# Halved 64-wide joins, blocks placed by ScalarE and DMA, and a recut second inversion in a delta-rule block kernel

## The reference, cut to what matters

```python
qkv = x @ gates_w + gates_b
q, k, v = jnp.split(qkv, 3, axis=-1)
lr = x @ lr_w + lr_b
k = k / jnp.linalg.norm(k, axis=-1, keepdims=True)
K = jnp.tril(jnp.einsum('ntc,nsc->nts', k, k), k=-1)
A = K + jnp.eye(T, dtype=x.dtype)
u = jax.scipy.linalg.solve_triangular(A, v, lower=True)
score = jnp.einsum('nsk,ntk->nst', q, k)
y = jnp.einsum('nst,ntv->nsv', score, lr * u)
```

## Time and profile before

| | us |
|---|---|
| median of 3 runs | 202.74 (202.15 to 202.99) |
| the profiled execution | 201.71 |
| its span, first to last instruction | 199.8 |
| PE busy | 179.8 (90%) |
| DVE busy | 166.3 (83%) |
| ACT busy | 114.4 (57%) |
| mean granted PE clock | 0.993 of full speed |

### The profile page before, as it was taken

One profiled execution on the slowest core, in us unless ns is written; L12 is line 12 of the kernel. 1 busy time (PEld: TensorE's weight loads), 2 busy tenths in 40 slices (PEclk: granted clock), 3 DMA queues, 4 the chain that ended last, 5 costly groups with the idle time before them and its releaser, 6 DMA issues.

```text
span 199.8 us, 4189 instructions
## 1 busy us (share of the span) xinstructions
PE 179.8 (90%) x1299; PEld 130.7 (65%) x1299; DVE 166.3 (83%) x750; ACT 114.4 (57%) x318; POOL 63.7 (32%) x79
## 2 busy tenths in 40 slices
PE   0498799999999899999998999999999999999980
PEld 0355676887988677877864776766667675657540
DVE  7898899999899945494686688898989899878885
ACT  2567786588795785457327763645456363752420
POOL 8256980000000069980022220070605233202030
PEclk9999999999999999999999999999999999999997
DMA  4982011103000030000000000010101001011011
GB/s 115 302 211 29 10 16 20 21 5 59 3 2 3 0 61 1 3 3 3 0 2 0 3 0 0 0 54 3 53 0 36 18 5 53 0 53 53 0 54 53
DMA packets 20265, 6.53 MB, mean 33 GB/s; under 512 B 9995, under 2 KB 20244, under 8 KB 20244
## 3 DMA queue, kind: packets, MB, share of 16 engines
q1 hardware_dynamic: 19668, 6.21, 13.1%
q10 hardware_dynamic: 576, 0.07, 0.2%
HBM read 3.15 MB, written 2.10 MB: 26 GB/s over the span
## 4 chain that ended last, share of the span: by engine, by line
PE 62%; DVE 17%; ACT 5%; issue 3%; DVEq 0%; ACTq 0%
PE ps L1390 25%; PE ps L1104 10%; PE ps L1298 5%; PE ps L1099 5%; PE ps L1369 4%; DVE kT_all L1022 3%; DVE xi L836 3%; DVE prod L829 3%; PE ps L1133 2%; PE ps L1288 2%; DVE rv L885 2%; PE ps L1226 2%; PE ps L1282 2%; PE ps L1213 2%; PE ps L1116 1%
## 5 line engine op out<-in xcount | busy, mean ns | idle before, releaser
L1390 PE MATMUL ps<-ewC,kT_all 128*128 128x256 f32 (+2 forms) x192 | 62.0, 455 | 0.7 <-DVE kT_all L1022 0.7
L1022 DVE COPY_PREDICATED kT_all<-mask,ps 128x256 f32<-128x256 int32 x112 | 49.1, 439 | 2.6 <-DVE mask L1008 0.3
L1390 PEld LDWEIGHTS ps<-ewC,kT_all 128*128 128x128 f32 x192 | 33.9, 190 | 16.6 <-issue 6.0
L359 POOL TENSOR_TENSOR x_all<-x_all,kT_all 128x512 f32<-128x512 f32 (+1 forms) x8 | 9.6, 1204 | 54.6 <-ACT kT_all L679 54.6
L836 DVE TENSOR_TENSOR xi<-xi,prod 128x60 f32<-128x60 f32 (+13 forms) x116 | 19.6, 207 | 0.3
L829 DVE TENSOR_TENSOR prod<-lts,xi 128x60 f32<-128x60 f32 (+13 forms) x116 | 19.3, 204 | 0.3
L353 POOL TENSOR_TENSOR x_all<-x_all,h_all 128x512 f32<-128x512 f32 (+1 forms) x9 | 10.3, 1150 | 24.6 <-DVE h_all L954 19.9
L1298 PE MATMUL ps<-ww,k_all 128*128 128x256 f32 (+1 forms) x72 | 17.1, 365 | 0.4 <-DVE ww L939 0.4
L322 POOL TENSOR_SCALAR h_all<-x_all,mv,rr 128x128 f32<-128x128 f32 x18 | 14.6, 822 | 7.5 <-DVE rr L751 7.5
L649 ACT ACTIVATE k_all<-h_all,nb,rr 128x128 f32<-128x128 f32 x32 | 13.4, 483 | 1.9 <-DVE nb L975 1.5
L336 POOL TENSOR_SCALAR bob<-bob 128x128 f32<-128x128 f32 x1 | 0.5, 528 | 42.5 <-DVE da_all L859 42.5
(11 more groups left out here) (156 smaller groups left out, 389.9 us busy)
## 6 DMA issues: line engine op xcount, KB each, us to landing
x_all<-in_L_attn_x_dram SPq DMA_DIRECT2D x7, 256.0 KB, 5.4
out_dram<-x_all SPq DMA_DIRECT2D x7, 256.0 KB, 2.3
ew<-in_L_ffn_expert_w_dram SPq DMA_DIRECT2D x1, 512.0 KB
gd<-gg_all SPq DMA_DIRECT2D x26, 16.0 KB, 1.8
tt_all<-dT_all SPq DMA_DIRECT2D x8, 48.0 KB, 2.1
x_all<-in_L_attn_x_dram SPq DMA_DIRECT2D x2, 128.0 KB, 2.8
out_dram<-x_all SPq DMA_DIRECT2D x2, 128.0 KB, 1.8
da_all<-d_all SPq DMA_DIRECT2D x4, 48.0 KB, 2.1
```

What stands on the lines that cost most here:

```text
L1022: nc.vector.copy_predicated(sel[t % 2][:, n], mask[t % 2][:, n, E - 1 - e].unsqueeze(2).broadcast_to([P, 2, F]), expert(e)).then_inc(picke ...
L1390: last = nc.tensor.matmul(dst, x1T[t % 2][:, 2 * pair + n], ewC[:, of], start=True, stop=True)
```

## The change

1. **Halved joins.** `y64_` and `t12` issue two products of 32 moving columns for each n in place of one of 64. In `y64_` both halves use the same 64 rows of the array and the same stationary block, and write to partitions 0-63 and 64-127 of bank 7. In `t12` they use rows 0-63 and rows 64-127, and write to banks 6 and 7. `y64` and `da_all` get 128 partitions for this. The copy of `y64_` becomes 128 partitions x 128 elements (before 64 x 256). `za` gets a fourth product for each n, which writes a second copy of its result to partitions 96-127, and a third ACT instruction.
2. **Placing.** DVE's `place` goes away. ACT places blocks 1 and 3 turned in `odd_place`, and block 0 plain in `plain_place`. SP issues eight DMAs for a group where it issued six, in another order; five of them now carry the first tile's blocks too (32 x 16 x 32). The first of them waits for `d_done` and the rest for `dT_done`.
3. **The second inversion** is cut at columns 12 and 23 (before 10 and 22), and `rv_all(3)` stands ahead of `plain_(1)`, not behind `turned(1)`.
4. **Order on PE and ACT** around tiles 0, 1 and 4, with waits to fit: `ya(t)` waits for `t12(t-1)` being copied.

The core of the diff:

```diff
-        da_all = sb("da_all", [2 * Q, T, NS, 2 * Q])
+        da_all = sb("da_all", [P, T, NS, 2 * Q])
-        y64 = [sb(f"y64{s}", [2 * Q, NS, 2 * Q]) for s in range(2)]
+        y64 = [sb(f"y64{s}", [P, NS, Q]) for s in range(2)]
...
@@ sync
+                sp.wait_ge(d_done, g + 1)
+                dst, src = plain(1, 1, 0)
+                sp.dma_start(dst, src).then_inc(rest_sent[g], 16)
                 sp.wait_ge(dT_done, g + 1)
...
-                for (dst, src), sent in ((turned(1), odd_sent), (turned(3), odd_sent), (plain(0), even_sent),
-                                         (turned(2), even_sent), (plain(1), rest_sent), (turned(0), rest_sent)):
+                for (dst, src), sent in ((turned(2, 0), two_sent), (turned(0, 0), rest_sent), (plain(0, 2, 0), rest_sent),
+                                         (plain(1, 3, 0), rest_sent), (turned(1, 1), odd_sent), (turned(3, 1), odd_sent),
+                                         (plain(0, 0, 1), zero_sent)):
...
@@ scalar
-            def turned_place(g, b):
+            def odd_place(g):
                 act.wait_ge(dT_done, g + 1)
                 act.wait_ge(tt_clear, 2)
-                r = slice(Q * b, Q * b + Q)
-                nc.scalar.copy(by_block(tt_all, g, r, b, 0, 1), dT_all[g][r, 0:NS]).then_inc(tt_act, 1)
+                for b in (1, 3):
+                    r = slice(Q * b, Q * b + Q)
+                    last = nc.scalar.copy(by_block(tt_all, g, r, b, 0, 1), dT_all[g][r, 0:NS])
+                last.then_inc(tt_act, 1)
...
+                for b in (1, 3):
+                    r = slice(Q * b, Q * b + Q)
+                    last = nc.scalar.mul(da_all[r, t, :, 0:Q],
+                                         ps[r, 6, 2 * NS * Q:3 * NS * Q].rearrange("p (n c) -> p n c", n=NS), -1.0)
+                last.then_inc(za_ready, 1)
...
-            plain_place(1)
-            turned_place(1, 2)
-            turned_place(1, 0)
...
@@ vector
-            place(0)
             prepare(1)
-            eliminate(1, 0, 10)
+            eliminate(1, 0, 12)
...
-            eliminate(1, 10, 22)
+            eliminate(1, 12, 23)
             rv_all(2)
-            eliminate(1, 22, Q - 1)
+            eliminate(1, 23, Q - 1)
+            rv_all(3)
             plain_(1)
             turned(1)
-            rv_all(3)
-            place(1)
...
@@ tensor
             def ya(t):
                 if t % TG == 0:
-                    pe.wait_ge(tt_dve, t // TG + 1)
+                    pe.wait_ge(tt_act, 2 * (t // TG) + 2)
...
+                joined(pe, t12_ready, t)
...
             def y64_(t):
...
+                pe.wait_ge(two_sent[t // TG], 16)
                 for n in range(NS):
-                    last = nc.tensor.matmul(ps[0:2 * Q, 7, 2 * n * Q:2 * (n + 1) * Q], gg_all[2 * Q:4 * Q, t, n, 0:2 * Q],
-                                            tt_all[2 * Q:4 * Q, t, n, 2 * Q:4 * Q], start=True, stop=True)
+                    for h in range(2):
+                        last = nc.tensor.matmul(ps[2 * Q * h:2 * Q * h + 2 * Q, 7, n * Q:n * Q + Q], gg_all[2 * Q:4 * Q, t, n, 0:2 * Q],
+                                                tt_all[2 * Q:4 * Q, t, n, (2 + h) * Q:(3 + h) * Q], start=True, stop=True)
                 last.then_inc(y64_mm, 1)
 
             def t12(t):
...
+                pe.wait_ge(rest_sent[t // TG], 16 * 4)
                 for n in range(NS):
-                    last = nc.tensor.matmul(ps[0:2 * Q, 7, 2 * (NS + n) * Q:2 * (NS + n + 1) * Q], da_all[:, t, n],
-                                            y64[t % 2][:, n], start=True, stop=True)
+                    for h in range(2):
+                        r = slice(2 * Q * h, 2 * Q * h + 2 * Q)
+                        last = nc.tensor.matmul(ps[0:2 * Q, 6 + h, (3 * NS + n) * Q:(3 * NS + n + 1) * Q], da_all[r, t, n],
+                                                y64[t % 2][r, n], start=True, stop=True)
                 last.then_inc(t12_mm, 1)
```

More of the change, by code:

```diff
@@ L169, in delta_block_kernel @@
         dT_done, d_done, nk_done = sem("dT_done"), sem("d_done"), sem("nk_done")
-        odd_sent, even_sent, rest_sent = [[sem(f"{name}_sent{g}") for g in range(NG)] for name in ("odd", "even", "rest")]
+        odd_sent, zero_sent, two_sent, rest_sent = [[sem(f"{name}_sent{g}") for g in range(NG)]
+                                                    for name in ("odd", "zero", "two", "rest")]
         prep_mm, prep_ready = sem("prep_mm"), sem("prep_ready")
-        tt_act, tt_dve = sem("tt_act"), sem("tt_dve")
+        tt_act = sem("tt_act")
         ya_mm, yb_mm, za_mm, zb_mm, y64_mm, t12_mm = (sem("ya_mm"), sem("yb_mm"), sem("za_mm"), sem("zb_mm"),
@@ L506, in y64_ @@
                 act.wait_ge(y64_mm, t + 1)
[L507 removed]
+                nc.scalar.copy(rows(y64[t % 2][:, :, :]), ps[:, 7, 0:NS * Q]).then_inc(y64_ready, 1)
             def t12(t):
                 act.wait_ge(t12_mm, t + 1)
[L511 to L512 removed]
+                nc.scalar.mul(tt_all[0:2 * Q, t, :, 2 * Q:4 * Q].rearrange("p n (h c) -> p h n c", h=2),
+                              ps[0:2 * Q, 6:8, 3 * NS * Q:4 * NS * Q].rearrange("p h (n c) -> p h n c", n=NS),
                               -1.0).then_inc(t12_ready[0], 1)
@@ L535, in _ @@
             v_(4)
+            plain_place(0)
             k_(7)
-            plain_place(0)
+            odd_place(0)
             ya(0)
@@ L612, in _ @@
                 lrw(t, 3)
-                za(t + 1)
-                s_(t, 0)
                 if t == TG - 1:
+                    s_(t, 0)
+                    odd_place(1)
                     s_(t, 1)
+                    plain_place(1)
+                    ya(t + 1)
+                    za(t + 1)
                     y64_(t + 1)
                 else:
+                    za(t + 1)
+                    s_(t, 0)
                     y64_(t + 1)
@@ L910, in _ @@
             rv_all(1)
-            eliminate(1, 10, 22)
+            eliminate(1, 12, 23)
             rv_all(2)
-            eliminate(1, 22, Q - 1)
+            eliminate(1, 23, Q - 1)
+            rv_all(3)
             plain_(1)
             turned(1)
-            rv_all(3)
-            place(1)
+            norms(1)
             yb(TG)
-            norms(1)
+            dve.wait_ge(nk_done, NG)
+            for n in LOW:
+                rv_(TG, n)
             zb(TG)
-            dve.wait_ge(nk_done, NG)
+            for n in HIGH:
+                rv_(TG, n)
+            t12(TG)
             dve.wait_ge(xT_mm, T)
-            rv_all(TG)
-            t12(TG)
             for t in range(TG, T):
@@ L1271, in _ @@
             y64_(0)
-            ya(1)
             pe.wait_ge(k_ready, T)
@@ L1308, in _ @@
                 w_(0, n)
+            za(1)
+            pe.wait_ge(v_ready, T)
+            for n in LOW:
+                s_(0, n, FIRST)
             y64_(1)
-            pe.wait_ge(v_ready, T)
-            for n in range(NS):
+            for n in HIGH:
                 s_(0, n, FIRST)
@@ L1314, in _ @@
             for t in range(1, T):
-                for n in range(NS):
+                for n in LOW:
                     ks(t, n)
                 if t == TG:
+                    za(t)
+                for n in HIGH:
+                    ks(t, n)
+                if t == TG:
+                    y64_(t)
                     t12(t)
@@ L1341, in _ @@
                 if t + 1 == TG:
-                    y64_(t + 1)
+                    ya(t + 1)
                 else:
```

70 lines of the change are left out of this document (24 added, 46 removed).

## The result

The changed kernel took 210.07 us (median of 4 executions, 206.37 to 212.31) against 202.44 us (201.68 to 202.99) for the kernel before (4 executions), 3.8% more by the medians. I forecast 204.1, and 206.0 was the top of my range. As the clock is what differs, I also count the executions whose mean granted clock is under 0.985.

What follows compares the result with a forecast made beforehand. PE was taken as the limit after tile 4: w_(4) starts 1.41 us later, the 6.25 us period stays, so +1.4 on the median of 202.74 gives 204.1 us. Range 200.8 to 206.0, the forecast's own 203.0 to 205.4.

Steps and rivals of the forecast that it cites:

- From tile 4 on: Scan from tile 4, where PE alone is the limit: its period stays at 6.25 us.
- change of group: From w_(3) to w_(4): 8.86 us where it was 7.32, so w_(4) starts at 78.74, +1.41.
- the wait of ya(5): Ahead of w_(4): ya(5), 0.37 us, waits for t12's copy on DVE, 0.5, where it ran beside it.
- The halved products: y64_ and t12 blocks of 0.60 us: saving 0 taken, with 0.21 off and 0.45 on as ends.
- the middle case: Weight load paces the halved products; a pair side by side takes one present product's time, saving 0, at most 0.03 us.
- Rival 1: Halves are paced by streaming: 0.21 us off each block on the path, 201.1 us; chance 0.27.
- Rival 2: Weight loads queue in y64_: 7 blocks at +0.45 us and the 1.4, 207.3 us; chance 0.07.
- blocks of 1 us: Sign in the y64_ and t12 blocks that the halves' weight loads queue, against 0.57 to 0.61 us if forecast right.
- The start and DVE's waits: Up to ks(1) and on DVE: ks(1) at 55.27 where it was 54.53; idle 1.5 us ahead of rv_all(1).
- Rival 3: The new order costs nothing: +0.1 is left of the +1.4, 202.8 us; chance 0.18.
- a wait on PE: DVE's saving in the second inversion becomes waiting: rv_all(3) starts at 69.43 behind ks(3), dT_done at 72.3, before 69.72.

Runs made afterwards that it cites:

- x_narrow: Changed kernel with narrower half-products in tiles 1 to 7: y64_ streams 16 columns for 32, t12 takes 32 stationary for 64; 208.28 us (one execution).
- x_whole: Changed kernel with the joins' products 64 columns wide again, without the two DMAs, za product and copy that only the halves need; 210.56 us.
- x_rvback: Changed kernel with rv_all(3) behind turned(1) again, as before the change; 204.25 us, ratio to before 1.0095.
- x_fill: Changed kernel with four idle products on PE ahead of ya(4) and four ahead of ya(5); 204.93 us, ratio to before 1.0142.
- x_yalate: Changed kernel with ya(5) behind w_(4) on PE, and its copy likewise on ACT; 212.30 us, ratio to before 1.0366.
- x_tgorder: Changed kernel with the old order at the change of group on PE, ACT and DVE; 202.55 us, ratio to before 1.0017.
- x_fillB: Changed kernel with four idle products on PE behind t12(4) and none ahead of ya(4); 204.83 us, ratio to before 1.0140.
- x_fillA: Changed kernel with four idle products on PE ahead of ya(4) alone; 208.77 us, ratio to before 1.0099.
- b_tglate: Kernel before with only the late order of tile 4's joins on PE, ACT and DVE; 203.09 us, ratio to before 1.0052.

## Why the prediction was wrong, point by point

The step that failed is "From tile 4 on. PE's period stays at 6.25 us". It took PE's clock for given. In its place the runs showed 11.16 us for the first period, at half clock, and 5.7 us more than before behind w_(4). The sums that lead up to it were nearly all right; one term of the change of group was too small, the wait of ya(5). Times of the changed kernel less 0.85 for its later turned(0):

| step | forecast | measured |
|---|---|---|
| y64_ and t12 block | 0.57 to 0.61 | 0.59 |
| ya(0) | 46.28 | 46.28 |
| t12(0) | 49.87 | 49.87 |
| ks(1) | 55.27 | 55.40 |
| rv_all(1), idle ahead of it | 55.91, 1.5 | 56.03, 1.70 |
| ks(3), rv_all(3) | 68.79, 69.43 | 69.04, 69.57 |
| turned(1) done | 72.3 | 72.45 |
| w_(3) | 69.88 | 70.04 |
| t12(4) | 77.3 | 77.39 |
| w_(4) | 78.74 | 79.84 |
| the first period behind it | 6.25 | 11.16 |

- **The halved products** give nothing back: the middle case, on L1159. Shown by x_narrow (half the stationary columns took 0.22 us off a block, half the moving ones 0.02) and x_whole. Rival 1 falls. Rival 2 falls too: its sign, blocks of 1 us, does stand in the trace (85.28 to 86.28), but only at the half clock; at full clock the block is 0.59.
- **The start and DVE's waits**: right to 0.2 us.
- **The change of group** came out 0.94 longer than my 8.86 (70.89 to 80.69). About 0.6 of it is a wait for DMAs, 0.2 is ya(5) at half clock (0.57 in place of 0.37), and the rest my other pieces. I had followed rest_sent to t12(4) and not odd_sent to ya(5). The two odd DMAs are the sixth and seventh of eight, issued from 75.97 on, and ya(5) waited for them until 80.12, 0.8 behind the end of t12(4)'s copy (78.94 + 0.42, less a little). The longest landing of the changed kernel's placing DMAs took 3.4 us, where the median is 2.2. In x_whole and x_rvback, without that wait, w_(3) to w_(4) is 79.24 - 70.15 = 9.09 and 79.07 - 70.08 = 8.99.
- **The clock**: 5.7 us of 9.1, in no term, no bound and no rival. That it is the clock, and that idle time on PE brings it, is shown by x_fill (0 of 6, where x_whole and x_yalate on the same chip fell in 11 of 12). That the order at the change of group opens these gaps is shown by x_tgorder (0 of 12, against 9 of 19 on its chip). No single gap is needed: the clock fell ahead of the second stretch in x_fillB, without the first in x_fillA, and without a wait for DMAs in x_whole and x_rvback. How much each weighs stays open: the counts are too small, and those of x_fillA, x_fillB and x_rvback can't be held against the changed kernel's 4 of 4, which come from another batch.
- **Rival 3** falls: the order costs 0.5% alone (b_tglate), and 2.5 us up to w_(4) with its waits.
- **Where the clock stayed**, the forecast of 204.1 us was good: 203.79 in x_whole, 203.7 to 204.3 in x_rvback, 203.9 and 204.4 in x_fillA.
- The part of the change that helps, the cuts, I saw only as "a wait on PE". By itself it is worth 0.7%.

## What to carry to other kernels

When a change makes a PE that was nearly always busy (9.54 of 10 us here) wait for others in a chain of small steps, price two things: the waits, and the clock of the work behind them. Here w_(4) came 2.5 us later, and the half clock behind it cost 5.7 us more. Idle products in the gaps tell the two apart. And where several DMAs are reordered, follow each semaphore to its waiter, the last in the queue first.

## What the runs showed of the hardware

- PE's granted clock fell from 2.4 to 1.2 GHz in the changed kernel though no gap ahead of it was over 1 us (0.92, 0.36, and the first 0.5 of the 1.22 us gap in which it fell). It stayed low for 10 to 27 us in the profiled executions that show it (10.2 in x_fillA's, 13.7 in the changed kernel's, 27.3 in x_fillB's), though in the changed kernel's PE was full again from w_(4) on.
- The same kernel does and doesn't show it from one execution to the next: x_whole took 203.8 us once and 210 to 216 five times.
- The fall comes at different places of the same stretch: at 77.3 us in x_fillB's and x_narrow's profiled executions, 79.4 in the changed kernel's, 80.8 in x_fillA's and 81.8 in x_yalate's.
- At half the clock a y64_ block takes 1.00 us (85.28 to 86.28), not twice 0.59.
- A pair of 64-wide weight loads on the same rows and different columns of the array costs what one does: the y64_ block takes 0.59 us with eight pairs and 0.60 with eight single records.
